# x, h and the normed output split in token order and turned by the DMA queue instead of TensorE

## What is computed

```
xn = layernorm(x)                        # x: 2 x 2048 tokens of 512
# attention: ternary weights, chunks of 128 tokens with a decaying state
h = rmsnorm(xn) * qkv_norm_w
q, k, v = split(h @ ternary(qkv_w).T)
o = scale * (decayed scores @ v + decayed q @ state), per chunk and head
y = rmsnorm(rmsnorm(o) * norm_w) * proj_norm_w
attn = y @ ternary(proj_w).T
# mixture of experts over all 4096 tokens, on the same xn
routed = top 2 of 8 experts by softmax(xn @ w_gate): silu(g) * u, then w_down
shared = (silu(xn @ wg) * (xn @ wu)) @ w_sh_down
out = x + attn + routed + shared
```

## Time and profile before

| | |
|---|---|
| median of 3 runs | 1407.35 us (1406.62 to 1409.09) |
| the profiled execution's own time | 1409.07 us |
| its span, first to last instruction | 1407.3 us |
| mean granted TensorE clock | 0.975 of full |
| busy share PE / DVE / ACT / POOL | 91% / 50% / 37% / 37% |

### The profile page before, as it was taken

How to read it: one execution, slowest core, us unless ns; L and a number is a source line. 1 busy time by engine, 2 the same in 40 slices (tenths; PEclk the granted TensorE clock), 3 DMA queues, 4 the chain that set the end, 5 groups by cost and what they waited for, 6 DMA issues and landing times. The chain is left out here.

```text
span 1407.3 us, 29711 instructions
## 1 busy us (share of the span) xinstructions
PE 1283.0 (91%) x10418; PEld 882.1 (63%) x10419; DVE 697.8 (50%) x1606; ACT 514.2 (37%) x1034; POOL 527.2 (37%) x467
## 2 busy tenths in 40 slices
PE   1599999999999994999999969999999969999997
PEld 1477777767776673777777734444444447777775
DVE  4477877878778775873333322222222213333323
ACT  3444444444444434433232324444444411111111
POOL 0333344333443332025450034445454542444333
PEclk9799999999999997999999989999999989999999
DMA  5213433334333344434542357887777761443333
GB/s 172 95 63 127 168 128 108 113 131 153 144 108 108 130 147 156 162 106 95 141 109 91 33 149 188 183 183 182 189 183 183 186 194 55 181 170 135 134 135 120
DMA packets 174061, 194.87 MB, mean 138 GB/s; under 512 B 100977, under 2 KB 107249, under 8 KB 174001
## 3 DMA queue, kind: packets, MB, share of 16 engines
q1 hardware_dynamic: 158464, 156.17, 36.6%
q0 software_dynamic: 13328, 37.04, 10.5%
q10 hardware_dynamic: 2208, 0.82, 0.2%
HBM read 117.55 MB, written 56.77 MB: 124 GB/s over the span
## 5 line engine op out<-in xcount | busy, mean ns | idle before, releaser
L1269 PE MATMUL gu<-xT,WG 128*128 128x256 f16 x3072 | 351.2, 275 | 24.0 <-PEq L1780 12.0
L1269 PEld LDWEIGHTS gu<-xT,WG 128*128 128x128 f16 x3072 | 303.2, 99 | 75.9 <-DVE WD L1556 12.8
L1280 PE MATMUL rgu<-WG,raw 128*128 x876 | 215.3, 383 | 20.1 <-issue 20.0
L1695 DVE SCALAR_TENSOR_TENSOR actv<-gu,up_inv,sg 128x512 f32<-128x512 f32 x64 | 48.1, 751 | 251.1 <-ACT sg L1532 250.9
L1532 ACT ACTIVATE sg<-gu,gate_inv 128x512 f32<-128x512 f32 x64 | 43.9, 686 | 320.0 <-PE gu L1269 320.0
L1280 PEld LDWEIGHTS rgu<-WG,raw 128*128 128x128 f16 x876 | 86.2, 98 | 111.2 <-issue 28.5
L1287 PE MATMUL yp<-WD,ah 128*128 128x512 f16 x512 | 152.3, 379 | 1.1 <-DVE al L1700 1.1
L1850 POOL TENSOR_TENSOR xsp<-xg,xsp 128x512 f16<-128x512 f32 x75 | 86.7, 1156 | 111.0 <-ACT xsp L1918 111.0
L655 PE MATMUL ring<-hh,qkvT 128*128 128x256 f16 x512 | 117.1, 277 | 6.0 <-DVE hl L972 6.0
L1250 POOL DMA_INDIRECT xg<-xn_dram,idx x77 | 73.8, 958 | 123.9 <-POOL xsp L1850 66.4
L655 PE MATMUL ring<-hl,qkvT 128*128 128x256 f16 x512 | 117.0, 276 | 0.0
(11 more groups left out here) (238 smaller groups left out, 2167.1 us busy)
## 6 DMA issues: line engine op xcount, KB each, us to landing
y_dram<-raw SPq DMA_DIRECT2D x72, 256.0 KB
xl<-in_L_attn_x SPq DMA_DIRECT2D x16, 512.0 KB, 4.4
xn_dram<-xn SPq DMA_DIRECT2D x16, 512.0 KB, 6.3
wraw<-in_L_ffn_w_gate_up SPq DMA_DIRECT2D x16, 512.0 KB, 6.8
xT_dram<-x SPq DMA_DIRECT2D x16, 512.0 KB, 2.8
xr<-in_L_attn_x SPq DMA_DIRECT2D x16, 512.0 KB, 5.7
x_dram<-x SPq DMA_DIRECT2D x32, 256.0 KB, 2.1
xT<-xT_dram SPq DMA_DIRECT2D x16, 512.0 KB, 6.3
```

What stands on the lines that cost most here:

```text
L1269: ins = pe.matmul(gu[:, h, f * tokens:(f + 1) * tokens], w[:, kk, b, a0:a0 + P], x[:, kk, a], start=(kk == 0 and (a, b) == PASSES[0]), sto ...
L1280: ins = pe.matmul(gu[bank][:], x(kk, a), w[:, 0, kk, b, :], start=(i == 0), stop=(i == len(done) - 1))
L1695: v.scalar_tensor_tensor(out=actv[:, g % 2], in0=gu[g % 2][:, 1].rearrange("p (f t) -> p f t", f=FT), scalar=up_inv[:, 1:2], in1=sg[:], op ...
```

## The change

- `xn` is split in token order: ScalarE writes `xs[:, u, 0]`, GpSimd `xs[:, u, 1]`. h is weighted in token order by GpSimd (`weighted_h`, new) with a broadcast weight `hw_b`, then split by ScalarE and VectorE into `hs`. The attention output is split in token order into `ys`.
- TensorE's `xn_turn` and `o_turn` go. Six transposing DMAs a step on SyncE's queue take their place: `turn_h`, `turn_x`, `turn_y`, two each. ScalarE's copies `take_xnT` go.
- `h_high` and `h_low` of chunk n+2 are now done at the end of step n, where before those of chunk n+1 were done at the start of it.
- `xs_dram` (both halves, f16) takes the place of `xn_dram`; its rows have the same 2 KB. The routed gather brings rows that are ready to turn, with four buffers instead of two, by an index that is read straight from `slots`; ScalarE's and GpSimd's split and VectorE's index copies go from that block, and SyncE's and GpSimd's loops there are written out.
- The turned x has another layout, so that the moving operand of the shared blocks' matmuls and of q and k is two runs of 128 columns instead of one of 256.

```diff
 class Ring:
-    STEP = ["xnT0", "xnT1", "kTr0", "ot0", "kv0", "q0", "q1", "kTr1", "ot1", "rt", "onT0", "k0", "kv1", "k1", "proj0",
-            "onT1", "v0", "v1", None, None, "proj1"]
+    STEP = ["kTr0", "ot0", "kv0", "q0", "q1", "kTr1", "ot1", "rt", "k0", "kv1", "k1", "proj0", "v0", "v1", "proj1"]
...
+            def turn_h(q, par):
+                n = 2 * q + par
+                if not (isinstance(n, int) and n == 0):
+                    wait_apart(sp, S["v_ready"], 2 * n, S["sp_passed"])
+                for u in range(B):
+                    wait_apart(sp, S["hl_ready"], 2 * n + u + 1, S["sp_passed"])
+                    sp.dma_start_transpose(hT[:, u], hs[:, u].rearrange("p a c -> p (a c)")).then_inc(hT_in[u], 16)
...
             def step(q, par, front, norm):      # SyncE
                 n = 2 * q + par
+                if front:
+                    turn_h(*after(q, par))
+                    turn_x(*after(q, par))
...
+                    store_xs(*after(q, par))
+                    store_xT(*after(q, par))
                 for u in range(B):
+                    turn_y(u, q, par)
+                store_x1(0, q, par)
...
             def h_high(q, par):                 # ScalarE
                 n = 2 * q + par
+                for u in range(B):
+                    act.wait_ge(S["hn_ready"], 2 * n + u + 1)
+                    act.wait_ge(hT_in[u], 16 * n)
+                    act.activation(hs[:, u, 0], hn[:, u], ACT.Copy).then_inc(S["hh_ready"], 1)
...
             def step(q, par, front, has_norm):  # VectorE
...
                 second_norm(1, q, par)
+                y_low(1, q, par)
                 weight_maxima(q, par, (0,))
                 if front:
                     decayed_scores(0, *nxt, (0, 1))
                 residual(0, q, par, st)
                 if has_norm:
                     norm(q + 1, par)
-                y_low(1, q, par, st)
                 if front:
                     decayed_scores(0, *nxt, (2, 3))
                 else:
                     weight_scales()
+                if has_norm:
+                    h_low(q + 1, par)
                 residual(1, q, par, st)
                 if has_norm:
                     norm_factors(q + 1, par)
...
+            def weighted_h(q, par):             # GpSimd
+                n = 2 * q + par
+                for u in range(B):
+                    pool.wait_ge(S["xn_ready"], 2 * n + u + 1)
+                    if not (isinstance(n, int) and n == 0):
+                        pool.wait_ge(S["hl_ready"], 2 * n + u - 1)
+                    pool.tensor_tensor(hn[:, u], xn[:, par, u], hw_b[:], ALU.mult).then_inc(S["hn_ready"], 1)
...
                 weighted(1, q, par)
                 update(1, q, par)
+                if norm:
+                    weighted_h(q + 1, par)
```

More of the change, by code:

```diff
@@ L616, in _ @@
         def _(pe):
[L617 to L625, removed]
             def router(q, par, st):
                 n = 2 * q + par
-                pe.wait_ge(S["xlow_ready"], n + 1)
+                for u in range(B):
+                    pe.wait_ge(xT_in[u], 16 * (n + 1))
                 bank, done = fill(pe, "rt", st)
@@ L641, in project @@
                 n = 2 * q + par
-                pe.wait_ge(S["h_ready"], n + 1)
+                for u in range(B):
+                    pe.wait_ge(hT_in[u], 16 * (n + 1))
                 bank, done = fill(pe, name, st)
@@ L946, in norm @@
                 v.wait_ge(S["rstd_ready"], n + 1)
-                v.wait_ge(xn_out[par], 16 * q)
+                if not (isinstance(n, int) and n < 2):
+                    v.wait_ge(S["xlow_ready"], 2 * n - 2)
                 for u in range(B):
@@ L1713, in step @@
                                  unit_experts)[i]()
-                            if half == 0 and last and g == 1:
-                                v.wait_ge(slot_in, 16)
-                                index(v, 0, 0)
-                                index(v, 0, 1)
                         if last:
@@ L1751, in _ @@
                                     in_=payload[:, kk, t, :], in_offset=None).then_inc(slot_out, 16)
-                        for par in range(2):
-                            gather(pool, 0, par, S["pool_passed"])
+                        pool.wait_ge(split, PIECES * (GROUPS + EXPERTS - 1))
+                        pool.wait_ge(slot_in, 16)
+                        for r in range(XG):
+                            gather(pool, r)
                         return
@@ L1799, in routed @@
                 block = c.enter_context(nc.Block())
-                def later(q, par, tiles):
-                    return q + (par + tiles) // 2, (par + tiles) % 2
                 def run_steps(eng, step):
@@ L1816, in _, with turn @@
                     load_tokens(sp, 1, 0, HALF)
-                    def turn(r, i):
-                        if not (isinstance(r, int) and r < XH):
+                    def turn(r):
+                        if r >= XH:
                             wait_apart(sp, S["gu_full"], r - XH + 1, S["sp_passed"])
-                        wait_apart(sp, S["low_ready"], r + 1, S["sp_passed"])
-                        sp.dma_start_transpose(xh[:, i % XH], xsp[:, i % 2].rearrange("p a c -> p (a c)")
-                                               ).then_inc(turned[i % 2], 16)
@@ L1831, in _ @@
                     for r in range(3):
-                        turn(r, r)
-                    for r in range(XH):
-                        turn(r + 3, r + 3)
-                        store(r, r % 2)
-                    with sp.Fori(1, SLOT_TILES // XH) as h:
-                        for i in range(XH):
-                            turn(XH * h + i + 3, i + 3)
-                            store(XH * h + i, i % 2)
+                        turn(r)
+                    for r in range(SLOT_TILES):
+                        if r + 3 < TURNS:
+                            turn(r + 3)
+                        store(r)
@@ L1855, in _ @@
-                    for r in range(3):
-                        low_part(r // 2, r % 2)
-                    def step(q, par, first):
-                        low_part(*later(q, par, 3))
-                    run_steps(pool, step)
-                    pool.wait_ge(xg_in[0], 16 * (SLOT_TILES // 2 + 3))
-                    pool.wait_ge(xg_in[1], 16 * (SLOT_TILES // 2 + 2))
+                    for r in range(XG, TURNS):
+                        pool.wait_ge(turned[r % XH], 16 * ((r - XG) // XH + 1))
+                        gather(pool, r)
@@ L1904, in some @@
                         for i in range(UNROLL):
-                            tile(UNROLL // 2 * h + i // 2, i, first and i == 0, places)
+                            tile(h, i, first and i == 0, places)
                     some(0, True)
```

295 lines of the change are left out of this document (127 added, 168 removed).

## The result

The changed kernel takes 1434.57 us (median of 4 runs, 1431.44 to 1436.98) against 1407.61 for the kernel before beside it: 1.0192 times as long, 95% interval 1.0179 to 1.0205. That is outside my range, though on the side that I held likelier (0.42). The profiled execution (the longest of the four, 1436.98 us) has a span of 1435.2 us, 27.9 over before, and a mean granted clock of 0.955 against 0.975.

The account below looks back on a forecast made before the run. TensorE was taken to bound attention and the routed block. Fourteen steps (+3.5), the last but one (-0.5), the start (-1) and the routed start (-0.5) sum to +1.5 on 1407.35: 1409 us, range 1395 to 1430.

Parts of the forecast that it names:

- the side that I held likelier (0.42): Whole kernel: a time slower than the 1404.5 to 1410.2 us counted as same, chance 0.42 (faster 0.33, same 0.25).
- TensorE's 2.8 us a step: Attention step: what TensorE alone would lose without the transposes of xn and y and one 0.87 us pause.
- The order of the chain: Attention step, VectorE: low y, maxima, xn, h's subtraction, second residual, factors, k scaling, first decay; K+17.1 without any hindrance.
- the port: Attention step: VectorE and GpSimd exclude each other on SBUF; factors end 1.1 us later, y wins against the state addition.
- the resume time: Attention step: TensorE resumes with the scores of batch 1 at K+18.1 instead of K+17.8, +0.35 us.
- K: Attention step: zero point of the predicted times, the read-out of k0, at 212.44 us in the kernel before.
- a few such falls: Attention steps with a 2.4 us pause: TensorE's clock falling to 0.50 adds +5 to +10 us in all.
- The first rival: Attention: state addition wins the port from low y (+22 us), or pauses cost clock (+5 to +10); 1430 us, chance 0.22.
- The bound of -0.25 a step: Attention step: its change of time, -0.25 us, if the factors have no port wait.
- the walk: Attention step: predicted VectorE sequence from the read-out of k0 to the same point a step later, +0.25 us a step.
- The queue's rival: Attention: the queue is 2 to 3 us later than can be swallowed, +1 us a step, 1421 us, chance 0.08.
- behind the same 1 MB of loads: Routed block's start: first turn issued 1 us sooner but behind those loads, -0.5 of the 10.91 us.

Follow-up runs that it names:

- e8: Changed kernel with y alone turned by TensorE again and split from PSUM, h and x still turned by the queue: 1435.36 us, ratio 1.0191.
- e1: Changed kernel with 18 useless matmuls a step ahead of the scores of batch 1, where TensorE waits for VectorE: 1416.73 us, ratio 1.0065.
- e6: Changed kernel with norm factors ahead of the norm of x, xl's load ahead of h's and x's turns, y's first turn ahead of two stores: 1396.16 us.
- e5: Changed kernel with the norm factors moved on VectorE from behind the second residual to ahead of the norm of x: 1420.98 us, ratio 1.0097.
- e7: Changed kernel with one more gather, which nothing reads, at the very end of the routed block: 1442.64 us, ratio 1.0263.
- e3: Changed kernel with 18 useless matmuls ahead of batch 1's scores and y's first turn ahead of two stores: 1421.3 us, ratio 1.009.

## Why the prediction was wrong

**What held.** TensorE's 2.8 us a step did turn into two pauses that VectorE ends. The order of the chain, the port (factors stretched by GpSimd's split, y ahead of the state addition) and the resume time were right to 0.15 us. h and x make the loss: with y undone it is the same (e8).

**The step that failed** is the sum of "The port" part: "So TensorE's scores resume at K+18.1, not K+17.8: +0.35", followed by a price for the rest of the step as though TensorE still ran at full speed. I had seen, the clock at half behind a pause of 3.0, and put it into a rival as "a few such falls", +5 to +10 in all. Measured, it is at 11 of 14 outer products, and worth 17.8 us net by the medians (e1), or 25.4 from chunk 0 to chunk 14 in the two traces (451.1 - 425.7). The gap between the two has two parts: e1 gives back 2.6 at its start, where the fillers find no pause, and the traced executions lie further apart (1436.98 and 1415.13) than the medians. The first rival named 1430 us for a mixture of clock and lost port. That it is near the time is luck: the 22 us in it are the price of y losing the port, which didn't happen, and the clock, which did, had only 5 to 10.

**What was mis-sized.** Of the 13.5 us that e1 still has over the kernel before in those 14 steps, 9.2 are 14 x (30.12 - 29.46), where I had 3.5. The resume time is 0.14 late, and that is a slip of mine: the successor of the second residual at K+14.9 and 0.87 for the factors make K+15.8, not the K+15.6 of the port part, and the sum is then K+18.2, as measured. And of the 0.6 by which scores behind the decay are stretched (1.37 for 0.74) I counted 0.3. Of the other 4.3, 2.2 are its two steps with the clock at 0.95 and most of the rest its early steps, which are the queue's part. The bound of -0.25 a step "without any port wait" doesn't follow from the walk either: K+17.1 against K+17.8, and the same -0.1, make -0.8; the nearest run is e6 with -0.4 (29.05 - 29.46), with the factors moved. The queue's rival (0.08, +1 a step) is true of the first four steps only (y is 0.9, 1.5, 3.0 and 1.0 late there), and it left out xl, which is late in the same steps and in every step once the chain is shorter (e5).

**What I missed.** The end of the routed block: -8.7 (e7). I read the earlier trace rows as "behind the same 1 MB of loads" for its start and didn't look at its end at all, where TensorE idled 11.97 and no other engine had work for most of it. Without this gain the change would have cost about 36 us (27.0 + 8.7).

**Left open.** When the clock falls. In the changed kernel pauses of 1.88 and 1.87 at the end of the first two steps leave it at 1.00; it falls behind 1.66 at the end of the third, and behind 1.97 later; e3 falls behind 1.27, and e6 holds with 0.92 and 1.27 in a step. The length of one pause doesn't decide it. Nor did I run the routed part alone, so its -8.7 is shown in the changed kernel, not as an edit of the kernel before; and why a late gather holds the block's end is not shown.

## What to carry to other kernels

Work taken from the bounding engine can be worth nothing while the engine behind it hands over in a fixed order: here it became two pauses, and the clock fell behind one of them, so that a step which was relieved of 2.8 us became 2.8 us longer (1.8 of it in the stretch that the fillers won back, 25.4 / 14). So first find what ends each pause that the change would open, and move what stands ahead of it (here six tiny factors, one maximum, one load and one turn; 1434.6 to 1379.6 us together). Use fillers as a probe: useless work in a pause tells at once how much of the loss is clock. And read the hand-overs between blocks as closely as the loops.

## What was unexpected of the hardware

- The same kernel got faster by 17.8 us with 288 useless matmuls in it (e1).
- With a gather as the last work of a block, the next block starts only 10 to 11 us after its issue, about 6 us of that with the DMA queues idle; with the last gather 26 us ahead of the next block TensorE's pause is 3.24 (e7).
- VectorE and GpSimd made each other wait in both directions: `rc` took 1.13 beside GpSimd's split of x and 0.22 without it (e6), and GpSimd's state addition took 1.67 beside the low half of y against 1.27. The Trainium skill (SBUF — State Buffer, "Who interferes with whom") says that whichever of two contending instructions is issued first gets the shared port pair for the whole instruction and the other is blocked; both places agree with it.
